# Second normalisation of a two-layer convolution kernel: tile 1 taken in four stretches of rows instead of in one piece

## The reference

```python
def _gn(v, G=32, eps=1e-05):
    g = v.reshape(B_, H_, W_, G, C_ // G)
    m = jnp.mean(g, axis=(1, 2, 4), keepdims=True)
    s = jnp.var(g, axis=(1, 2, 4), keepdims=True)
    return ((g - m) / jnp.sqrt(s + eps)).reshape(v.shape)
...
x = x + _L0_conv_ref(_gn(x), ...)   # 5 steps of a diffusion stencil, batch norm, ReLU
x = x + _L1_conv_ref(_gn(x), W, b)  # 3x3 convolution with ternary weights, ReLU
```

## Time and profile before

| | us |
|---|---|
| three runs, median (lowest to highest) | 279.26 (278.02 to 279.52) |
| the profiled execution, its own time | 277.91 |
| its span in the trace | 276.1 |
| PE busy | 233.6 (85%) |
| DVE busy | 247.2 (90%) |
| ACT busy | 133.8 (48%) |

### The profile page before, as it was taken

One profiled execution on the slowest core, in us unless ns is written; L12 is line 12 of the kernel. 1 busy time (PEld: TensorE's weight loads), 2 busy tenths in 40 slices (PEclk: granted clock), 3 DMA queues, 4 the chain that ended last, 5 costly groups with the idle time before them and its releaser, 6 DMA issues.

```text
span 276.1 us, 5235 instructions
## 1 busy us (share of the span) xinstructions
PE 233.6 (85%) x2276; PEld 209.6 (76%) x2276; DVE 247.2 (90%) x196; ACT 133.8 (48%) x207; POOL 16.8 (6%) x36
## 2 busy tenths in 40 slices
PE   0137999999959999279999999999999987889793
PEld 0136889989925588279989999898989986767683
DVE  3799999999999989999998999999999989886821
ACT  3294776879860054702623425160603246917743
POOL 2000000003310201101000101010101000000000
PEclk9999999999979999959999999999999999999999
DMA  6950000005998771990700334248610030000124
GB/s 213 350 116 0 0 4 6 2 0 112 199 205 253 152 152 38 209 209 2 154 0 2 76 78 94 61 116 190 129 26 1 0 138 17 2 0 0 62 93 152
DMA packets 7190, 24.94 MB, mean 90 GB/s; under 512 B 2816, under 2 KB 3328, under 8 KB 5120
## 3 DMA queue, kind: packets, MB, share of 16 engines
q0 software_dynamic: 2304, 14.68, 26.6%
q1 hardware_dynamic: 4720, 9.61, 10.6%
q10 hardware_dynamic: 144, 0.33, 0.4%
HBM read 6.79 MB, written 2.10 MB: 32 GB/s over the span
## 4 chain that ended last, share of the span: by engine, by line
DVE 54%; PE 27%; issue 9%; ACT 7%; DMA 1%; DVEq 0%; ACTq 0%
DVE ring L918 24%; DVE coef L653 8%; PE psum L1180 8%; PE psum L1170 6%; ACT coef L380 5%; PE psum L1257 5%; DVE first_two L1004 4%; PE psum L1117 3%; PE psum L1087 3%; DVE state L729 2%; DVE coef L964 1%; DMA bn<-in_norms 1%; DVE ring L722 1%; DVE hi_s L734 1%; DVE gsum L687 1%
## 5 line engine op out<-in xcount | busy, mean ns | idle before, releaser
L918 DVE TENSOR_TENSOR ring<-coef,state 128x2048 f32<-128x2048 f32 x51 | 113.5, 2286 | 2.1 <-PE psum L1180 1.9
L1180 PE MATMUL psum<-mats,ring 128*128 128x128 f32 x816 | 96.6, 278 | 9.6 <-DVE ring L918 9.5
L1180 PEld LDWEIGHTS psum<-mats,ring 128*128 128x128 f32 x816 | 91.4, 144 | 13.3 <-DVE ring L918 12.9
L380 ACT ACTIVATE state<-psum 128x1024 f32<-128x1024 f32 x36 | 35.1, 1028 | 74.3 <-PE psum L1180 60.2
L653 DVE SCALAR_TENSOR_TENSOR coef<-coef 128x2048 f32<-128x2048 f32 x16 | 36.4, 2290 | 0.7 <-issue 0.2
L380 ACT ACTIVATE coef<-coef 128x2048 f32<-128x2048 f32 (+1 forms) x10 | 17.6, 1783 | 10.1 <-DMA coef<-coef 9.9
L1257 PE MATMUL psum<-hi,dense_m 128*128 128x512 f32 (+1 forms) x54 | 20.0, 379 | 0.9 <-ACT coef L380 0.9
L1139 PEld LDWEIGHTS psum<-coef,state 32*128 32x128 f32 x672 | 19.4, 187 | 1.4 <-issue 1.3
L380 ACT ACTIVATE coef<-psum 128x512 f32<-128x512 f32 (+2 forms) x23 | 17.5, 766 | 5.4 <-PE psum L1117 4.3
L1139 PE MATMUL psum<-coef,state 32*128 32x64 f32 x672 | 20.0, 271 | 0.0
L1257 PE MATMUL psum<-lo,dense_m 128*128 128x512 f32 (+1 forms) x54 | 19.5, 369 | 0.0
(11 more groups left out here) (133 smaller groups left out, 280.4 us busy)
## 6 DMA issues: line engine op xcount, KB each, us to landing
first_two<-coef POOLq DMA_DIRECT2D x7, 1024.0 KB, 8.5
coef<-coef POOLq DMA_DIRECT2D x5, 1024.0 KB, 8.8
coef<-in_x SPq DMA_DIRECT2D x2, 1024.0 KB, 6.0
coef<-in_wide_taps SPq DMA_DIRECT2D x3, 384.0 KB, 7.6
ring<-in_x SPq DMA_DIRECT2D x2, 512.0 KB, 6.0
ring<-in_x SPq DMA_DIRECT2D x1, 1024.0 KB, 10.3
coef<-coef SPq DMA_DIRECT2D x1, 1024.0 KB, 7.6
out<-coef SPq DMA_DIRECT2D x2, 512.0 KB, 3.1
```

The lines of the kernel that those rows point to most:

```text
L380: return nc.scalar.activation(dst, src, func, **kw)
L918: V.tensor_tensor(wc(ring[:, slot, :]), wc(coef[:, t, a, :]), h_at(t, k, dw, dc), ALU.mult)\
L1180: ins = mm(slot_ap(name)[:, (j % 8) * 128:(j % 8) * 128 + 128], src[:, j * 128:j * 128 + 128], ident, is_transpose=True, start=first and j ...
```

## The change

Four things change, all in the tail.

1. Tile 1's `normalise`, the rounding and the lower part are cut at pair rows 5, 9 and 13 into four stretches (5, 4, 4 and 4 of the 17 rows). Each of the eight pieces is cut with them: DVE now issues 20 piece instructions where it issued 5, and ACT 12 where it issued 3. ACT still rounds stretches 1, 2 and 3 (a function `upper_rows`); stretch 0 is rounded by DVE itself (`first_upper_rows`). `dense(1, i)` waits for stretch min(i, 3).
2. On ACT the root of tile 1 (`rsqrt_first`) stands ahead of `relu_dense(0,0)`, and so do its pieces of stretch 0. `relu_dense(0,1)` stands behind the rounding of stretch 1, `take_out(0,0)` behind that of stretch 3.
3. On DVE the second lower part of tile 0 (8 pair rows) moves from ahead of `residual(1)` to behind `spread(1)`. `output_sum(0,0)` stands ahead of the lower part of stretch 1, `output_sum(0,1)` behind that of stretch 3.
4. On PE `dense(1,0)` stands ahead of `out_natural(0,0)`, and `group_var2(1)` is let in after matmul 21 of `dense(0,0)` instead of 22.

```diff
+        row_cuts = ((0, PAIRS // 2 + 1, PAIRS + 1), (0, 5, 9, 13, PAIRS + 1))
+
+        def pieces_through(pieces, t, c):
+            return len(pieces[0]) + len(pieces[1]) * (c + 1) if t else len(pieces[0])
...
+        def piece_of(ap, t, k, b, c, shifted_by):
+
+            j0, j1 = (0, PAIRS) if t == 0 else (max(row_cuts[1][c] - k, 0), min(row_cuts[1][c + 1] - k, PAIRS))
+            return ap.rearrange("p (j h b) -> p j h b", b=BT, h=H)[64 * (k ^ shifted_by):64 * (k ^ shifted_by) + 64,
+                                                                   j0 + k * shifted_by:j1 + k * shifted_by, :, b]
...
+            def upper_rows(t, c):
 
                 act.wait_ge(pads_ready, 4)
                 act.wait_ge(edges_ready, 2 * (t + 1))
+                act.wait_ge(xn_ready, pieces_through(act_pieces, t, c))
+                act.wait_ge(xn_too, pieces_through(dve_pieces, t, c))
+                if t:
+                    wait_job(act, "cf_0_1")
+                copy(by_rows(hi[:, :], t, c)[:, :, BT:BT + 128], by_rows(odd_pairs(t), t, c)).then_inc(xh_ready, 1)
...
             relu_bn_out(1, 0)
             relu_bn_out(1, 1)
+            rsqrt_first(128, BT)
+            normalise(1, 0)
             relu_dense(0, 0)
-            rsqrt_first(128, BT)
-            normalise(1)
-            upper_half(1)
+            normalise(1, 1)
+            upper_rows(1, 1)
             relu_dense(0, 1)
+            normalise(1, 2)
+            upper_rows(1, 2)
+            normalise(1, 3)
+            upper_rows(1, 3)
             take_out(0, 0)
...
+            def first_upper_rows():
+
+                dve.wait_ge(edges_ready, 4)
+                dve.wait_ge(xn_ready, pieces_through(act_pieces, 1, 0))
+                dve.wait_ge(xn_too, pieces_through(dve_pieces, 1, 0))
+                wait_job(dve, "cf_0_0")
+                then(V.tensor_copy(by_rows(hi[:, :], 1, 0)[:, :, BT:BT + 128], by_rows(odd_pairs(1), 1, 0)))
...
-            lower_half(0, 0)
-            lower_half(0, 1)
+            lower_rows(0, 0)
             residual(1)
             spread(1)
+            lower_rows(0, 1)
             ask_norm(1)
             second_norm(1)
-            normalise(1)
+            normalise(1, 0)
+            first_upper_rows()
+            lower_rows(1, 0)
+            normalise(1, 1)
             output_sum(0, 0)
-            lower_half(1, 0)
-            lower_half(1, 1)
+            lower_rows(1, 1)
+            normalise(1, 2)
+            lower_rows(1, 2)
+            normalise(1, 3)
+            lower_rows(1, 3)
             output_sum(0, 1)
...
             dense(0, 0, 0, 18)
             group_mean2(1)
-            dense(0, 0, 18, 22)
+            dense(0, 0, 18, 21)
             group_var2(1)
-            dense(0, 0, 22)
+            dense(0, 0, 21)
             dense(0, 1)
+            dense(1, 0)
             out_natural(0, 0)
-            dense(1, 0)
             dense(1, 1)
```

More of the change, by code:

```diff
@@ L68, in job_table @@
         jobs += halves(f"acc_{k}", t)
-    jobs += [("mean2_1", 0), ("var2_1", 1), ("cf_0_0", 2), ("cf_0_1", 3), ("tb_0_0", 0),
-             ("cf_1_0", 2), ("cf_1_1", 3), ("tb_0_1", 1), ("cf_1_2", 0), ("tb_1_0", 2), ("cf_1_3", 1), ("tb_1_1", 2),
+    jobs += [("mean2_1", 0), ("var2_1", 1), ("cf_0_0", 2), ("cf_0_1", 3), ("cf_1_0", 2),
+             ("tb_0_0", 0), ("cf_1_1", 3), ("tb_0_1", 1), ("cf_1_2", 0), ("tb_1_0", 2), ("cf_1_3", 1), ("tb_1_1", 2),
              ("cf_1_4", 3), ("tb_1_2", 0), ("tb_1_3", 1), ("tb_1_4", 3)]
@@ L191, in by_rows @@
         def by_rows(ap, t, i):
-            first = first_rows[t]
-            return ap.rearrange("p (j r) -> p j r", j=PAIRS + 1)[:, slice(0, first) if i == 0 else slice(first, None)]
+            return ap.rearrange("p (j r) -> p j r", j=PAIRS + 1)[:, row_cuts[t][i]:row_cuts[t][i + 1]]
+        def piece_of(ap, t, k, b, c, shifted_by):
+            j0, j1 = (0, PAIRS) if t == 0 else (max(row_cuts[1][c] - k, 0), min(row_cuts[1][c + 1] - k, PAIRS))
+            return ap.rearrange("p (j h b) -> p j h b", b=BT, h=H)[64 * (k ^ shifted_by):64 * (k ^ shifted_by) + 64,
+                                                                   j0 + k * shifted_by:j1 + k * shifted_by, :, b]
         def slot_ap(name):
@@ L539, in relu_bn_out, with normalise @@
                            bias=outw[:, 3:4]), name)
-            def normalise(t):
+            def normalise(t, c=0):
                 act.wait_ge(norm_ready, t + 1)
-                x1 = coef[:, t, 2, :].rearrange("p (j h b) -> p j h b", b=BT, h=H)
-                to = odd_pairs(t).rearrange("p (j h b) -> p j h b", b=BT, h=H)
                 for k, b in act_pieces[t]:
                     p = slice(64 * k, 64 * k + 64)
-                    copy(to[64 * (1 - k):64 * (1 - k) + 64, k:k + PAIRS, :, b], x1[p, :, :, b], ACT.Identity,
+                    copy(piece_of(odd_pairs(t), t, k, b, c, 1), piece_of(coef[:, t, 2, :], t, k, b, c, 0), ACT.Identity,
                          scale=gn2[p, t, 3, b:b + 1], bias=gn2[p, t, 4, b:b + 1]).then_inc(xn_ready, 1)
-            def upper_half(t):
+            def upper_rows(t, c):
                 act.wait_ge(pads_ready, 4)
                 act.wait_ge(edges_ready, 2 * (t + 1))
[L555 to L560, removed]
+                act.wait_ge(xn_ready, pieces_through(act_pieces, t, c))
[3 more added lines that the diff above has]
+                copy(by_rows(hi[:, :], t, c)[:, :, BT:BT + 128], by_rows(odd_pairs(t), t, c)).then_inc(xh_ready, 1)
             def relu_dense(t, h):
@@ L956, in second_norm, with normalise, lower_rows @@
                        norm_ready, t + 1)
[L958 to L961 removed]
+            def normalise(t, c=0):
                 for k, b in dve_pieces[t]:
                     p = slice(64 * k, 64 * k + 64)
[L964 removed]
+                    V.tensor_scalar(piece_of(odd_pairs(t), t, k, b, c, 1), piece_of(coef[:, t, 2, :], t, k, b, c, 0),
                                     gn2[p, t, 3, b:b + 1], gn2[p, t, 4, b:b + 1], ALU.mult, ALU.add)\
                         .then_inc(xn_too, 1)
[L968 to L971, removed]
+            def first_upper_rows():
[4 more added lines that the diff above has]
+                then(V.tensor_copy(by_rows(hi[:, :], 1, 0)[:, :, BT:BT + 128], by_rows(odd_pairs(1), 1, 0)))
+            def lower_rows(t, c):
+                if (t, c) != (1, 0):
+                    dve.wait_ge(xh_ready, 2 * t + c + (1 - t))
+                V.tensor_tensor(by_rows(lo[:, :], t, c)[:, :, BT:BT + 128], by_rows(odd_pairs(t), t, c),
+                                by_rows(hi[:, :], t, c)[:, :, BT:BT + 128].bitcast(f32), ALU.subtract).then_inc(xl_ready, 1)
             def output_sum(t, h):
@@ L1246, in dense @@
                 begin, end = out_cuts[t][i:i + 2]
[L1247 removed]
+                pe.wait_ge(xl_ready, 2 * t + 1 + min(i, 3))
                 dst = take(f"cf_{t}_{i}") if first == 0 else slot_ap(f"cf_{t}_{i}")
```

4 lines of the change are left out of this document (2 added, 2 removed).

## The result

The changed kernel is slower: 282.92 us, median of 6 runs (281.67 to 284.19), against 279.28 (278.02 to 279.52, 6 runs) for the kernel before; ratio 1.016, 95% interval 1.0134 to 1.0185. The forecast was 279.9 with a range of 278.1 to 281.6, no change, with 0.20 on slower. The profiled execution took 282.84 us, with a span of 281.1 against 276.1. These two traces lie 5.0 us apart where the medians lie 3.6 apart: the profiled execution of the kernel before was one of its quick ones, 1.4 us under its median. What follows accounts for the two traces.

What follows compares the result with a forecast made beforehand. Bound: the wait chain to tile 1's normalisation, then PE's order, so when out_natural(0,1) starts. Pieces start 1.4 us earlier, but the late sum gives 263.9 - 263.3 = +0.6; 279.26 + 0.6 = 279.9 us, range 278.1 to 281.6.

Steps and rivals of the forecast that it cites:

- Root and lower part: Tile 1's statistics: lower part moved, group mean 0.35 us earlier, rs_in 0.1 later; root ahead of ReLU, pieces 1.4 earlier.
- matmul 21: On PE, letting group_var2(1) in after matmul 21 instead of 22 of dense(0,0) was to buy nothing.
- The shape of the walk: Tail: DVE's late sum starts out_natural(0,1) at 263.9; PE arrives at 261.1 and waits 2.8 us.
- Prices of the short instructions: Tile 1's stretches: 64x128 piece 0.32 us on DVE, 0.60 on ACT; DVE cast of 640 elements 0.48.
- upper bound, 265.5: Walk's end if pieces never overlap (DVE 0.37 us apart, ACT 0.63): 265.5, +2.2 us.
- rival 4: PE's clock falls at the stop ahead of out_natural(0,1), costing 1.5 us more: +2.1, 281.4 us; chance 0.08.
- stop of 2.8 us: PE's forecast wait ahead of out_natural(0,1), from 261.1 to 263.9, with no clock loss in the forecast.
- Rival 3: The short pieces on DVE and ACT are dear: beyond +1.4, up to +2.2 us, 280.7 to 281.5; chance 0.12.
- the forecast's net effect: Start of out_natural(0,1) moves from 263.3 to 263.9, and the end with it: +0.6 us.

Runs made afterwards that it cites:

- e4: The kernel before with only tile 0's second lower part on DVE moved from ahead of residual(1) to behind spread(1): 278.14 us, ratio 0.9981.
- e3: The kernel before with only tile 1's root moved ahead of relu_dense(0,0) on ACT: 277.11 us against 278.58, ratio 0.9944.
- e1: The changed kernel with output_sum(0,1) moved ahead of the lower part of stretch 2 on DVE: 279.93 us, ratio 1.0058 to the kernel before.
- e5: The changed kernel with output_sum(0,1) ahead of stretch 2's lower part, take_out(0,0) and relu_dense(1,0) ahead of ACT's stretch 3 pieces: 277.41 us, ratio 0.9962 to the kernel before.
- e6: The changed kernel with DVE's tile 1 pieces using constants instead of scale and shift read from SBUF: 281.26 us, one execution.
- e7: The changed kernel with tile 1 cut at pair rows 6, 10 and 14 instead of 5, 9 and 13: 282.38 us, one execution.

## Why the prediction was wrong

Point by point, by its own steps.

1. *Root and lower part.* Right. -0.35 at the group mean (e4: 0.35), `rs_in` 0.1 late all the same, pieces 1.5 earlier for 1.4 (e3: 1.5, of which 1.2 reach `out_natural(0,1)`). No gain from matmul 21 was forecast; no run has it alone.
2. *The shape of the walk.* Right: DVE's order decides when `out_natural(0,1)` starts, PE arrives there near 261 and stops. It is the step on which the forecast of "no gain" rested, and e1 and e5 show it by moving the sum. One wait was placed otherwise: DVE was to wait 1.2 us for ACT in stretch 2 and not in stretch 3; it waited 0.86 and 0.85.
3. *The prices on DVE.* This step failed first, in "Prices of the short instructions": a 64x128 piece was put at 0.32 us and took 0.39; it was interpolated to a four-element instruction with no pointer operands, and e6 shows that these are 0.12 of it. On ACT I had taken the ReLUs that carry the same two operands, and hit 0.60. Stretches 0, 1 and 3 took 0.40, 0.41 and 0.43 more; the cast 0.34 more (e7); and ACT waited 0.20 behind DVE's last piece where I had put 0.05. From the start of the pieces to the end of the sum it was 15.04 us against 13.24: 1.8 more. The prediction's upper bound, 265.5, is 14.9 us from the start of the pieces, so even that was passed: it let the pieces cost up to 0.37 apiece but left the cast at 0.48. The pieces do overlap, by 0.08; their fixed part was too small.
4. *The clock.* The mechanism stood in rival 4, with 1.5 us for 2.35 measured and a chance of 0.08. This is the second failed step and the larger one. A stop of 2.8 us was judged safe with one fall to go by, that at the stop of 3.12 us. The experiments show the clock fallen at stops of 2.46 (e6, transposes at 1.61 instead of 1.03), 2.71 (e1), 3.77, 4.12 and 4.20 us, and not at 0.77, 1.27, 1.38 and 1.66. So even at my prices, with a stop of 2.8, the fall would have been the likely case; e6, whose walk is nearly the forecast's, had it at 2.46. The price of 1.5 was too low as well. It came from a fall after which the clock was low for 3.4 us (79.0 to 82.4); in the changed kernel it was low for 6.8 (264.0 to 270.8), and PE worked through 4.9 of them at half rate. The trace of the kernel before holds a second fall that the prediction does not use, and by it the price would have been near:

```profile
116.00:118.00 2.00, 0.00 (x0) 0.00 (x0) 2.00 (x2) 0.00 (x0) 0.86 (x1) 0.64 0.96 197
...
122.00:124.00 2.00, 2.00 (x14) 2.00 (x14) 2.00 (x2) 0.00 (x0) 0.00 (x0) 0.65 1.16 238
```

PE stood 5.57 us until 118.96, and the clock was low from about 116.6 to 123.4: 4.4 us of work at half rate, an estimate of 2.2 us lost.

5. *The rivals.* Rival 3 (dear pieces) and rival 4 happened together, the first lengthening the stop for the second. They were priced as if either came alone; the forecast's own range ended below their sum.

Of the 5.0 us of the profiled pair, 0.25 lie ahead of the tail, 0.6 are the forecast's net effect, 1.8 the mis-sized prices and 2.35 the clock: 5.0. What stays open: the medians differ by 3.6 only, and no trace of an execution of the kernel before near its median shows which part is smaller there; and no run had a stop between 1.66 and 2.46 us in the tail.
